# A written-out order for five engines, a ring of three probability groups, and value products in pairs, in an attention and mixture-of-experts kernel

## The chip, the core and the metric

One Trainium2 chip, one core. The metric is device time in microseconds (us) of one execution. TensorE is called PE, VectorE DVE, ScalarE ACT, GpSimd POOL, and SyncE SP; SP issues nearly all transfers.

## The reference, cut to what matters

The input is 8 images of 128 channels by 1024 positions, all float32. Each image ("batch") goes through three stages:

```
x  = x + softmax(q k^T) v                      # one head, key width 16; q,k,v are 1x1 convolutions of x
a  = layernorm(x)                              # token by token
g  = 8-head attention over 1024 tokens (head width 16) of a
l  = 4-head attention over a window of 5 tokens of a
a1 = layernorm(a + silu([g, l] W1) W2);  a2 = layernorm(a1 + silu(a1 W3) W4);  t2 = a2 (with the added t)
```

After all batches every token goes to one of 8 experts (argmax of a gate, capacity 1280 per expert), `relu(x w1 + b1) w2 + b2`, times the gate's probability, is scattered back, and is added to t2.

## The kernel before, in words

The kernel has an opening (weights, the first image's convolution attention), a main stage in which eight batches overlap, a short end for the last batch, and the expert stage with the output. All engines run straight-line programs; what is planned is only the order in which each engine takes its pieces.

A piece is a named **step**, such as `max_pair` or `conv_pv`, with up to four engines that handle it one after the other: for `max_pair` PE fills a PSUM tile and DVE reduces it. `all_steps` (line 584) lists the steps by **chain**: head (convolution attention of a batch, its q, k and the window's rows), maxima, scores, tail (everything behind the attention), local (window attention), and smaller ones. Within a chain an engine keeps the listed order; how the chains are interleaved on an engine is free. Before, `Steps.plan` (line 309) did this at build time with a table of costs (`PARTS`, line 127), a list schedule and one pass that pulls work tight (`justified`); it also put idle matmuls (`end_keep_on`) into gaps of PE at the end.

For the eight-head attention a batch has two **quads** of four heads. Each quad takes 32 `max_pair` steps (line 1602: two fp16 matmuls into `max_ps`, then a DVE reduction over 1024 columns, line 2297), a `guard` that turns the maxima into a row to be subtracted, moved by a transfer (`guard_rows`, lines 1179 and 2309), and then 32 `score_pair` steps (line 1620: two fp16 matmuls into `score_ps`, then one exponential over 1024 columns on ACT into `prob`, line 1994). `max_ps` and `score_ps` are single buffers of two PSUM banks each, so PE can't fill the next pair before DVE or ACT has read this one. Two `score_pair` steps make a **group**: four heads by 512 queries for one block of 128 keys. A `pv_group` (line 1635) multiplies a group with the values: four heads, each on its own 32 columns of the array, float32, 8 matmul records, accumulated over 8 key blocks in `o_ps`; `o_copy` then takes the sum away. `prob` (line 738) holds two groups: the exponential of group g waits for the product of group g - 2 (line 1997).

On PE a batch has, beside these, 16 `conv_max`, 16 `conv_exp` and 8 `conv_pv` (line 1560: 16 matmul records each), 8 `local_qkv`, and the tail's steps (`fuse1`, `fuse2`, `ffn1`, `ffn2` and transposes). On DVE there are 64 maxima and 16 `conv_max` reductions (line 2239) in each batch besides. Head steps share two PSUM banks (three in the opening), tail steps one.

In the opening, ACT's `conv_exp` of the first batch waits for `fold` (line 1917), the last of the weight steps, since the weights are loaded over the tile (`nat`, line 806, inside `cprob`) that the exponentials overwrite. On SP `recall` of batch 0 (line 1132) stands between the two `store_parts` of batch 0 (line 1138), and one `zero_rows` (line 1111: 528 KB of `rows_d` and 512 KB of `y_d`) stands ahead of the first `guard_rows`, the other nine behind it.

Of the kernel before, what the change touches and what calls it, by code (L numbers as in the profile page):

```python
# [19 lines left out]

# [40 lines left out]
GROUPS = 2 * NT  # L61
TILES = GROUPS * QH
# [64 lines left out]
PARTS = {  # L127
    "score_pair": [("pe", 0.26, 0.25), ("act", 1.28, 0.1)],
    "pv_group": [("pe", 1.08, 0.25)],
    "weights": [("sp", 6.0, 9.0)],  # L130
    "weight": [("pe", 0.25, 0.3), ("dve", 0.25, 0.1)],
    "fold": [("pe", 1.6, 0.3), ("dve", 2.0, 0.2), ("act", 0.1, 0.2)],
    "zero_pads": [("sp", 1.8, 3.0)],
    "zero_rows": [("sp", 0.5, 4.0)],
    "o_copy": [("act", 0.55, 0.2)],
    "bounds": [("dve", 1.6, 0.2), ("pe", 0.45, 0.3)],
    "powers": [("dve", 0.5, 0.2), ("pool", 0.4, 0.2)],
    "scales": [("dve", 2.6, 0.2)],
    "max_pair": [("pe", 0.26, 0.25), ("dve", 1.13, 0.1)],
    "guard": [("dve", 0.7, 0.1), ("pe", 0.11, 0.3)],  # L140
    "guard_rows": [("dve", 0.2, 0.2), ("sp", 1.3, 3.5)],
    "load_x": [("sp", 0.4, 9.0)],
    "x_tokens": [("pe", 0.5, 0.3), ("act", 0.55, 0.1)],
    "conv_qk": [("pe", 0.9, 0.3), ("act", 1.12, 0.2), ("dve", 1.38, 0.1)],
    "store_parts": [("sp", 1.3, 4.3)],
    "conv_v": [("pe", 0.87, 0.3), ("dve", 0.6, 0.1)],
    "conv_max": [("pe", 0.22, 0.22), ("dve", 0.6, 0.1)],
    "conv_guard": [("dve", 0.7, 0.1), ("pe", 0.1, 0.3), ("act", 0.3, 0.2), ("sp", 0.7, 2.5)],
    "conv_exp": [("pe", 0.22, 0.22), ("act", 0.54, 0.1)],
    "conv_pv": [("pe", 1.85, 0.25), ("dve", 0.5, 0.1)],  # L150
    "a_channels": [("pe", 0.45, 0.3), ("act", 0.54, 0.1)],
    "keep": [("sp", 1.0, 4.0)],
    "global_qk": [("pe", 0.88, 0.3), ("act", 0.56, 0.2), ("dve", 0.69, 0.1)],
    "local_qkv": [("pe", 0.65, 0.3), ("dve", 0.5, 0.2), ("sp", 0.9, 2.5)],
    "key_stacks": [("sp", 1.9, 4.5)],
    "query_stacks": [("sp", 1.9, 3.2)],
    "global_v": [("pe", 0.88, 0.3), ("dve", 0.6, 0.1)],
    "o_tokens": [("pe", 0.46, 0.3), ("dve", 0.65, 0.1)],
    "o_channels": [("pe", 0.45, 0.3), ("act", 0.54, 0.1)],
    "recall": [("sp", 1.8, 8.0)],  # L160
    "bias": [("pool", 4.9, 0.2)],
    "local_dot": [("sp", 0.9, 6.0), ("pool", 3.6, 0.2)],
    "local_max": [("dve", 2.1, 0.2), ("act", 0.25, 0.2)],
    "local_sum": [("dve", 0.7, 0.2), ("pool", 2.55, 0.2)],
    "local_out": [("pool", 2.8, 0.2)],
    "fuse1": [("pe", 1.73, 0.3), ("act", 1.2, 0.1), ("dve", 0.75, 0.2)],
    "ffn1": [("pe", 0.88, 0.3), ("act", 1.2, 0.1), ("dve", 0.75, 0.2)],
    "fuse2": [("pe", 1.74, 0.3), ("dve", 0.6, 0.1)],
    "ffn2": [("pe", 1.74, 0.3), ("dve", 0.6, 0.1)],
    "stats_t": [("dve", 0.8, 0.1), ("pool", 3.1, 0.1)],  # L170
    "stats_u": [("dve", 0.8, 0.1), ("pool", 3.1, 0.1)],
    "stats_v": [("dve", 0.8, 0.1), ("pool", 3.1, 0.1)],
    "stats_t2": [("dve", 0.8, 0.1), ("pool", 3.1, 0.1)],
    "norm_t": [("act", 1.6, 0.1)],
    "norm_u": [("act", 1.6, 0.1)],
    "affine_u": [("pool", 2.6, 0.1)],
    "norm_v": [("act", 1.6, 0.1), ("pool", 2.6, 0.1)],
    "norm_t2": [("act", 1.6, 0.1)],
    "store_t2": [("sp", 0.4, 3.0)],
    "x1_channels": [("pe", 0.45, 0.3), ("act", 0.54, 0.1)],  # L180
    "n2_channels": [("pe", 0.45, 0.3), ("act", 0.54, 0.1)],
    "logits": [("pe", 1.75, 0.3), ("dve", 1.75, 0.2)],
    "ranks": [("pe", 0.4, 0.3), ("act", 0.3, 0.2), ("dve", 4.2, 0.2)],
    "route": [("pool", 10.2, 3.0)],
    "end_o_tokens": [("pe", 0.46, 0.3), ("dve", 0.65, 0.1)],
    "end_o_channels": [("pe", 0.45, 0.3), ("act", 0.54, 0.1)],
    "end_fuse1": [("pe", 1.73, 0.3), ("act", 0.55, 0.1), ("dve", 1.4, 0.2)],
    "end_fuse2": [("pe", 1.74, 0.3), ("dve", 0.6, 0.1)],
    "end_stats": [("dve", 1.5, 0.1), ("pool", 1.1, 0.1)],
    "end_norm_u": [("dve", 0.9, 0.1)],  # L190
    "end_centre": [("dve", 0.9, 0.1)],
    "end_affine_u": [("pool", 2.6, 0.1)],
    "end_x1_channels": [("pe", 0.45, 0.3), ("act", 0.54, 0.1)],
    "end_ffn1": [("pe", 0.88, 0.3), ("act", 0.55, 0.1), ("dve", 1.4, 0.2)],
    "end_ffn2": [("pe", 1.74, 0.3), ("dve", 0.6, 0.1)],
    "end_norm_v": [("dve", 0.9, 0.1)],
    "end_store": [("sp", 0.4, 3.0)],
    "end_norm_t2": [("dve", 0.9, 0.1)],
    "end_n2_channels": [("pe", 0.45, 0.3), ("act", 0.54, 0.1)],
    "end_logits": [("pe", 0.9, 0.3), ("dve", 1.6, 0.2)],  # L200
    "end_ranks": [("pe", 0.3, 0.3), ("act", 0.3, 0.2), ("dve", 3.2, 0.2)],
    "end_route": [("pool", 1.3, 3.0)],
}

READ_BY_ALL = {"conv_qk", "global_qk"}
BESIDES = {"pe": 0.0, "act": 0.0, "dve": 0.0, "pool": 0.0, "sp": 0.0}
EARLIER = {"head": 0.0, "maxima": 5.0, "scores": 0.0, "tail": 0.0, "local": 1.0}  # L210
TOGETHER = 0.05
GUARD_LANDS = 7.0
STACKS_LAND = 9.0

ZERO_PADS_FROM = 58.0
ZERO_ROWS_FROM = 150.0
FIRST_WEIGHTS, WEIGHTS = 3, 20
SHIFTS = [
]

KEEP_OVER = 0.6
KEEP_SHARE = 0.75
KEEP_EARLY_OVER = 0.35
KEEP_EARLY_SHARE = 0.45
KEEP_TAKES = 0.22
KEEP_AT_END = 40


def first_gap(starts, ends, at, time):

    n, end = 0, len(ends)
    while n < end:
        mid = (n + end) // 2
        if ends[mid] <= at + 1e-9:
            n = mid + 1
        else:
            end = mid
    while n < len(starts) and starts[n] < at + time - 1e-9:
        at = max(at, ends[n])
        n += 1  # L240
    return n, at


def packed(parts, waits, order, backwards):

    taken, at = {}, [0.0] * len(parts)
    for k in order:
        engine, time, arrives = parts[k][:3]
        if backwards:
            t = arrives + max([at[x] + parts[x][1] for x in waits[k]], default=0.0)  # L250
        else:
            t = max([parts[k][5]] + [at[x] + parts[x][1] + parts[x][2] for x in waits[k]])
        starts, ends = taken.setdefault(engine, ([], []))
        n, t = first_gap(starts, ends, t, time)
        starts.insert(n, t)
        ends.insert(n, t + time)
        at[k] = t
    return at


def justified(parts, before, opens, at):

    span = max(t + p[1] + p[2] for t, p in zip(at, parts))
    back = packed(parts, opens, sorted(range(len(parts)), key=lambda k: (-at[k] - parts[k][1], -k)), True)
    late = [span - t - p[1] for t, p in zip(back, parts)]
    return packed(parts, before, sorted(range(len(parts)), key=lambda k: (late[k], k)), False)


def shifted(parts, before, opens, at, what, batch, us):

    key = list(at)
    for k, (_, _, _, (b, step), chain, _) in enumerate(parts):
        if b == batch and what in (step[0], "chain " + chain):
            key[k] += us
        key[k] = max([key[k]] + [key[x] + 1e-6 for x in before[k]])
    at = packed(parts, before, sorted(range(len(parts)), key=lambda k: (key[k], k)), False)
    return justified(parts, before, opens, at)


class Steps:  # L280


    def __init__(self):
        self.steps = []
        self.found = {}
        self.uses = {}
        self.keep_from = None
        self.keeps_on = False
        self.early = False

    def add(self, chain, ahead, step, *before, banks=None, at=0.0):

        n = len(self.steps)
        deps = [(self.found[x], None) for x in before if x in self.found]
# [7 lines left out]
        self.steps.append((chain, ahead, step, deps, held, at))  # L302
# [6 lines left out]
    def plan(self):  # L309

        parts, before = [], []
        part_of, last_in, early, ready = {}, {}, [], []
# [27 lines left out]
        for k, b in enumerate(before):  # L340
            for x in b:
                opens[x].append(k)
# [2370 lines left out]
```

## Time and profile before

| | us |
|---|---|
| median of 3 runs | 1706.99 (1704.41 to 1714.14) |
| profiled execution | 1710.45 |
| its span, first to last instruction | 1708.7 |
| PE / DVE / ACT / POOL busy in the span | 1466.8 / 1251.4 / 994.1 / 715.1 |
| mean granted clock of PE | 0.912 of 2.4 GHz |

Busy time of PE is the union of matmul intervals with modelled ends, so a busy PE may still have room. The share of a whole span mixes stages; the rows further down are by stage.

### The profile page before, as it was taken

How to read it: one execution, taken by the hardware profiler on the slowest of the kernel's cores; microseconds unless marked ns; L12 is line 12 of the kernel's file. 1: busy time of each engine (PE TensorE's matmuls, PEld its weight loads, DVE VectorE, ACT ScalarE, POOL GpSimd, SP SyncE). 2: the span in 40 equal slices, each digit the busy share in tenths (PEclk: the TensorE clock that was granted, in tenths of full speed). 3: DMA queues.
4: the chain of work that ended last, by engine and by line, in shares of the span. 5: the costliest groups of instructions: out<-in, count | busy, mean ns of one | idle time of the engine just before them, and what ended most of it. 6: DMA issues, size and time to landing. Idle time of an engine off the chain costs nothing.

```text
span 1708.7 us, 23938 instructions
## 1 busy us (share of the span) xinstructions
PE 1466.8 (86%) x8489; PEld 691.9 (40%) x8489; DVE 1251.4 (73%) x2245; ACT 994.1 (58%) x1379; POOL 715.1 (42%) x1131
## 2 busy tenths in 40 slices
PE   6767888999999889988998899899978877879993
PEld 4513322543254335333533353245312321449992
DVE  5477688788867886798679867986777732648984
ACT  2302566676667666767576757666665665315543
POOL 5212411145444544454255425542653355224562
PEclk8956799999899999999999999999978965989997
DMA  2234531123212321332034203410421001033335
GB/s 73 95 101 159 193 93 49 40 98 101 81 45 98 98 88 41 101 116 73 35 112 136 72 5 112 147 52 9 157 93 49 35 35 46 7 88 108 107 119 211
DMA packets 111050, 148.40 MB, mean 87 GB/s; under 512 B 13558, under 2 KB 80171, under 8 KB 110932
## 3 DMA queue, kind: packets, MB, share of 16 engines
q1 hardware_dynamic: 103444, 136.69, 24.6%
q0 software_dynamic: 4608, 7.30, 1.3%
q10 hardware_dynamic: 2880, 2.88, 0.5%
q8 instruction: 68, 1.11, 0.3%
q14 instruction: 50, 0.41, 0.1%
HBM read 91.83 MB, written 56.95 MB: 87 GB/s over the span
## 4 chain that ended last, share of the span: by engine, by line
PE 55%; DVE 27%; issue 6%; ACT 6%; POOL 3%; DMA 2%; SPq 1%; POOLq 0%; ACTq 0%; DVEq 0%
DVE gmax L2297 14%; PE bank L1644 10%; PE max_ps L1610 7%; PE bank L1565 7%; PE score_ps L1631 5%; PE bank L1879 4%; PE bank L1681 3%; ACT prob L2000 3%; DVE cmax L2241 3%; PE bank L1671 2%; PE bank L1477 2%; PE bank L1581 2%; DVE stats L2269 2%; PE bank L1557 2%; PE bank L1700 1%
## 5 line engine op out<-in xcount | busy, mean ns | idle before, releaser
L2000 ACT ACTIVATE prob<-score_ps,unscale 128x1024 f32<-128x1024 f32 x512 | 569.3, 1112 | 346.6 <-PE score_ps L1631 345.0
L2297 DVE TENSOR_REDUCE gmax<-max_ps 128x2 f32<-128x1024 f32 x512 | 625.7, 1222 | 165.1 <-PE max_ps L1610 161.1
L1644 PE MATMUL bank<-prob,v_tok 128*32 128x512 f32 x2048 | 306.3, 674 | 1.5 <-ACT prob L2000 1.5
L1610 PE MATMUL max_ps<-arena 48*128 48x512 f16 x1024 | 213.9, 414 | 90.4 <-DVE gmax L2297 78.8
L1631 PE MATMUL score_ps<-arena 50*128 50x512 f16 x1024 | 212.6, 412 | 58.2 <-ACT prob L2000 56.3
L1610 PEld LDWEIGHTS max_ps<-arena 48*128 48x128 f16 x1024 | 50.1, 94 | 311.7 <-DVE gmax L2297 245.2
L1384 POOL TENSOR_TENSOR lprod<-ls,kv_win 128x640 f32<-128x640 f32 x64 | 80.0, 1273 | 227.6 <-DVE ls L2358 227.1
L1377 POOL TENSOR_TENSOR lprod<-ql_tok,kv_win 128x640 f32<-128x640 f32 x64 | 97.8, 1548 | 144.9 <-DMA ql_tok<-ql_d 143.9
L1631 PEld LDWEIGHTS score_ps<-arena 50*128 50x128 f16 x1024 | 50.3, 95 | 211.6 <-ACT prob L2000 159.2
L1565 PE MATMUL bank<-cv_tok,cprob 128*128 128x129 f32 x912 | 116.2, 280 | 1.6 <-DVE t_tok L2264 0.9
L1565 PEld LDWEIGHTS bank<-cv_tok,cprob 128*128 128x128 f32 x912 | 106.4, 191 | 21.8 <-issue 19.2
L1467 POOL DMA_INDIRECT y_d<-kv_win,token_e x80 | 82.6, 1033 | 75.9 <-DVE kv_win L2657 56.1
L1434 POOL DMA_INDIRECT rows_d<-rows,slot x56 | 55.2, 986 | 135.2 <-DVE slot L2457 120.2
L1342 POOL TENSOR_TENSOR mv<-stats 128x4 f32<-128x4 f32 x58 | 11.9, 204 | 197.4 <-DVE stats L2269 197.4
L1644 PEld LDWEIGHTS bank<-prob,v_tok 128*32 128x32 f32 x2048 | 42.2, 112 | 92.4 <-issue 81.2
L2241 DVE TENSOR_REDUCE cmax<-bank 128x1 f32<-128x512 f32 x107 | 71.9, 682 | 2.1 <-PE bank L1543 2.1
L1955 ACT ACTIVATE cprob<-bank 128x512 f32<-128x512 f32 x110 | 64.2, 597 | 9.9 <-PE bank L1557 9.8
L1351 POOL TENSOR_TENSOR rstd<-mv,half_pow 128x4 f32<-128x4 f32 x58 | 59.0, 1018 | 4.6
L1543 PE MATMUL bank<-ck_stack,cq_stack 128*128 128x512 f32 x107 | 56.3, 540 | 3.6 <-DVE cmax L2241 3.3
L2027 ACT ACTIVATE tanh_t<-bank,hcols 128x512 f32<-128x512 f32 x56 | 38.4, 687 | 32.1 <-PE bank L1671 20.9
L2363 DVE SCALAR_TENSOR_TENSOR hid<-tanh_t,half_t 128x512 f32<-128x512 f32 x56 | 48.3, 862 | 9.2 <-ACT half_t L1909 9.2
L1586 PE MATMUL bank<-lT,a_cm 128*128 128x384 f32 x118 | 54.7, 553 | 0.0
(399 smaller groups left out, 2496.7 us busy)
## 6 DMA issues: line engine op xcount, KB each, us to landing
kv_win<-kv_d SPq DMA_DIRECT2D x32, 1280.0 KB, 5.5
kv_d<-lqkv SPq DMA_DIRECT2D x64, 128.0 KB, 1.8
arena<-gparts_d SPq DMA_DIRECT2D x96, 64.0 KB, 2.6
rows_d<-rows SPq DMA_DIRECT2D x10, 528.0 KB, 6.9
cprob<-rows_d SPq DMA_DIRECT2D x8, 660.0 KB, 5.8
x_cm<-in_x_dram SPq DMA_DIRECT2D x8, 512.0 KB, 3.3
kept_d<-t_tok SPq DMA_DIRECT2D x8, 512.0 KB, 2.6
kept_d<-a_tok SPq DMA_DIRECT2D x8, 512.0 KB, 3.6
```

Of the source, the lines that this page charges most:

```text
L1377: m = pool.tensor_tensor(lprod[:, i, :, :], ql_tok[:, i, None, :].to_broadcast([P, WIN, C]), kv_win[:, i, :, 0:C], ALU.mult)
L1384: m = pool.tensor_tensor(lprod[:, i, :, :].rearrange("p w (h d) -> p w h d", d=LD), ls[:, i, :, :, None].to_broadcast([P, WIN, LH, LD]), k ...
L1467: pool.indirect_dma_start(y_d, bass.IndirectOffsetOnAxis(ap=token_e[e % 2][:, i:i + 1], axis=0), y_e[e % 2][:, i, :], None, bounds_check=l ...
L1565: last = mm(ps[:, 0:C + 1], conv_prob(b, i // HT)[:, j, (i % HT) * P:(i % HT + 1) * P], cv_tok[:, j, :], start=(j == 0), stop=(j == NT - 1))
L1610: last = mm(max_ps[:, z, :], q_stack[quad][Z * z:Z * z + CROWS, r, i * P:(i + 1) * P], key_slot(b, quad)[Z * z:Z * z + CROWS, r, j * HN:(j ...
L1631: last = mm(score_ps[:, z, :], key_slot(b, quad)[Z * z:Z * z + KM, r, j * P:(j + 1) * P], q_stack[quad][Z * z:Z * z + KM, r, half * HN:(ha ...
L1644: last = mm(o_ps[CG * h:CG * (h + 1), :], v_tok[:, j, quad * QH + h, :], prob[:, g % 2, h, :], start=(j == 0), stop=(j == NT - 1))
L1879: last = mm(bank[6 + u % 2][:, i * C:(i + 1) * C], hid_e[f][:, lo + i * P:lo + (i + 1) * P], w2_e[e % 2][:, f, :], start=(f == 0), stop=(f ...
L1955: nc.scalar.activation(conv_prob(b, h)[:, j, :], ps[:, :], ACT.Exp).then_inc(free, 1)
L2000: nc.scalar.activation(prob[:, g % 2, 2 * r:2 * r + 2, :], score_ps[:, :, :], ACT.Exp, scale=unscale[:, quad * PAIRS + r:quad * PAIRS + r ...
L2241: v.tensor_reduce(cmax[:, t // 2, t % 2:t % 2 + 1], ps[:, :], AX.X, ALU.max)\
L2297: v.tensor_reduce(gmax[:, :, r * NT + i, j:j + 1], max_ps[:, :, :], AX.X, ALU.max).then_inc(max_free, 1)
```

## The change

1. The planner with its costs goes. A table `ORDER` gives, for each engine, one letter per step: the chain whose next step the engine takes. `Steps.orders` expands it, `Steps.check` walks it once at build time. Idle matmuls at the end are the dots: 69 single ones in place of 12 steps of 3 to 21.
2. `prob` holds three groups (`PROB_RING = 3`), used in turn across quads and batches.
3. One `pv_group` takes two adjacent key blocks (`VALUES = 2`): 16 matmul records in a row, 8 such steps for each quad and 16 for each batch; they form a chain of their own, `values`. The exponential of group g now waits for the step that holds group g - 3.
4. `nat` moves from `cprob` to a part of `arena` that isn't used yet; `conv_exp` of batch 0 no longer waits for `fold`.
5. The early idle matmuls are deleted from the code (the order before holds none of them).

With the table some steps pass others on a queue. On SP, `recall` of batch 0 now stands behind both `store_parts`, and seven `zero_rows` stand ahead of the first `guard_rows`. On DVE the 16 `conv_max` of batch 1 come among the first twenty maxima, and the 8 `conv_pv` of batch 1 ahead of the first guard (four of them came behind it before).

```diff
+PROB_RING = 3
+VALUES = 2
+PRODUCTS = GROUPS // VALUES
...
+CHAINS = {"h": "head", "m": "maxima", "s": "scores", "t": "tail", "l": "local", "p": "split", "q": "queries",
+          "k": "keys", "x": "x", "z": "zero", "a": "end0", "b": "end1", "v": "values"}
+
+ORDER = {
+    "pe": (
+        "hhhhhhhhxhxhxhhhhhhhhhhhhhxxxxxxxxxxxxxhhhhhxhhhxhhhhhhhhhhxhhhhhhhhhhhhhhhthhhhthmhmmhmhmmhmhhmhhh"
+        "mhhhhhhhmhhmhhmhmmmhmmhhmhhhmhhhmhmhmhmhmhhmmmhhmhhmhhmhhmhhmhmmmhmhhmshmshmshmshmsvsmhhsmsmshmsvsmh"
...
+        "stmsmsvmstmsmstmsvmtsmtststsvstssssvsssvssstsvtstsstssvsssvssssvasasaasasaasvsasbbv...babaabba..b...."
+        "............b...bb..........ba...a...................ab...b..........b"
+    ),
...
+    "sp": (
+        "xxxhzhpptqkhhqxhhkhhqhhqlhlzzzzzzzmzhzzlppkxhhhhqlhhhhmqkhlqmhqppkxhhlhhqhhhlhmqkhttqlqmhlppkxlhhhhh"
...
-                      (a, ("pv_group", quad, n // PAIRS - 2)), banks=SCORE_PS)
-        if n % PAIRS == PAIRS - 1 and n >= PAIRS:
-            product(n // PAIRS - 1)
-    product(GROUPS - 1)
+        s.add("scores", a, ("score_pair", quad, n), (a, ("guard_rows", quad)), group(n // PAIRS - PROB_RING),
+              banks=SCORE_PS)
+        if (n + 1) % (VALUES * PAIRS) == 0:
+            product((n + 1) // (VALUES * PAIRS) - 1)
...
-        prob = sb("prob", [P, 2, QH, HN])
+        prob = sb("prob", [P, PROB_RING, QH, HN])
...
-        nat = cprob[:, :, :].rearrange("p a b -> p (a b)")
+        nat = arena[:, (QUADS + KEY_SLOTS) * N:]
...
+                for g in range(n * VALUES, (n + 1) * VALUES):
+                    j = g % NT
+                    for h in range(QH):
+                        last = mm(o_ps[CG * h:CG * (h + 1), :], v_tok[:, j, quad * QH + h, :], prob_of(b, quad, g)[:, h, :],
+                                  start=(j == 0), stop=(j == NT - 1))
...
-                if r == 0 and not (isinstance(b, int) and b == 0 and quad == 0 and g < 2):
-
-                    after(act, pv_made, b * 2 * GROUPS + quad * GROUPS + g - 1)
+                if r == 0:
+
+                    after(act, pv_made, ((2 * b + quad) * GROUPS + g - PROB_RING) // VALUES + 1)
```

## Rows read from the trace of the kernel before

**Rows 1.** Busy time by stage: stretch, its length, PE, PEld, DVE, ACT, POOL, clock, DMA.

```profile
0.00:89.00 89.00, 60.88 (x291) 42.21 (x291) 39.60 (x105) 24.89 (x45) 33.55 (x67) 0.87 0.30 88
89.00:163.00 74.00, 53.16 (x172) 21.83 (x170) 59.41 (x78) 4.66 (x10) 11.27 (x9) 0.58 0.32 105
...
784.00:951.00 167.00, 151.47 (x908) 65.17 (x908) 134.31 (x234) 114.06 (x159) 77.88 (x134) 0.98 0.25 83
...
1289.00:1424.00 135.00, 108.37 (x578) 35.39 (x578) 73.40 (x133) 86.94 (x111) 64.27 (x105) 0.80 0.15 49
...
1540.00:1662.00 122.00, 122.00 (x909) 114.52 (x908) 106.37 (x210) 62.43 (x114) 69.64 (x68) 1.00 0.39 115
```

**Rows 2.** Maxima (line 2297) and exponentials (line 2000): min/median/max ns, first and last start.

```profile
L2297 DVE TENSOR_REDUCE gmax<-max_ps x512: 1206/1225/1229, 89.5 to 1375.3; 128x2 f32<-128x1024 f32 x171
...
L2000 ACT ACTIVATE prob<-score_ps,unscale x512: 1092/1113/1137, 163.1 to 1462.7; 128x1024 f32<-128x1024 f32 x171
```

**Rows 3.** Waits in 453 to 1118 us: engine, line, releaser; total us, times, longest.

```profile
ACT prob L2000 <- PE score_ps L1631: 164.7, 148, 8.5
PEld max_ps L1610 <- DVE gmax L2297: 106.1, 148, 1.7
```

**Rows 4.** PE's timeline at full clock: start, us, line; turns, and a product alone.

```profile
254.14 0.39 PE L1610 MATMUL max_ps<-arena 48*128 48x512 f16 x2 [0.33 <-DVE gmax L2297]
254.37 0.38 PE L1631 MATMUL score_ps<-arena 50*128 50x512 f16 x2
254.68 0.91 PE L1586 MATMUL bank<-lT,a_cm 128*128 128x384 f32 x2
255.85 0.39 PE L1610 MATMUL max_ps<-arena 48*128 48x512 f16 x2 [0.27 <-DVE gmax L2297]
...
759.54 1.06 PE L1644 MATMUL bank<-prob,v_tok 128*32 128x512 f32 x8
760.54 0.39 PE L1631 MATMUL score_ps<-arena 50*128 50x512 f16 x2
```

**Rows 5.** PE's timeline: products side by side, and two alone at low clock.

```profile
1305.21 3.59 PE L1644 MATMUL bank<-prob,v_tok 128*32 128x512 f32 x16
...
1464.19 1.92 PE L1644 MATMUL bank<-prob,v_tok 128*32 128x512 f32 x16
...
1410.15 1.93 PE L1644 MATMUL bank<-prob,v_tok 128*32 128x512 f32 x8
...
1413.84 0.61 PE L1631 MATMUL score_ps<-arena 50*128 50x512 f16 x2 [1.21 <-ACT prob L2000]
1414.38 1.93 PE L1644 MATMUL bank<-prob,v_tok 128*32 128x512 f32 x8
```

**Rows 6.** DVE by line and shape, whole span: the reduction of `conv_max`.

```profile
L2241 DVE TENSOR_REDUCE cmax<-bank 128x1 f32<-128x512 f32 x107 | 71.9, 682 | 2.1 <-PE bank L1543 2.1
```

**Rows 7.** The chain of waits in the opening: start, us, what.

```profile
29.95 0.27 PE score_ps L1477
...
36.51 0.79 PE score_ps L1557
...
76.07 8.46 DMA gparts_d<-parts
```

**Rows 8.** SP's queue: start, us to issue, line, transfer.

```profile
73.43 0.64 SPq L1135 DMA_DIRECT2D t_old<-kept_d  x1
74.11 1.23 SPq L1136 DMA_DIRECT2D a_old<-kept_d  x1
75.44 1.31 SPq L1142 DMA_DIRECT2D gparts_d<-parts  x2
...
155.70 1.39 SPq L1183 DMA_DIRECT2D arena<-gneg_rows  x2
157.14 0.41 SPq L1113 DMA_DIRECT2D rows_d<-rows  x1
```

**Rows 9.** Busy time while zero rows are written; the last two columns DMA share, GB/s.

```profile
160.00:170.00 10.00, 7.48 (x42) 2.96 (x40) 8.68 (x18) 5.20 (x7) 3.25 (x12) 0.76 1.01 331
```

More of the change, by code:

```diff
@@ L21 @@
+from collections import deque
 from contextlib import ExitStack
@@ L120 @@
 TAIL_TURNS = len(TAIL_USES)
[L127 to L202, printed above, removed]
@@ new lines @@
+ENGINES = {
+    "load_x": "sp",
+    "weights": "sp",
+    "weight": "pe dve",
+    "fold": "pe dve",
+    "bounds": "dve pe",
+    "powers": "dve pool",
+    "scales": "dve",
+    "zero_pads": "sp",
+    "zero_rows": "sp",
+    "conv_qk": "pe act dve",
+    "x_tokens": "pe act",
+    "conv_v": "pe dve",
+    "conv_max": "pe dve",
+    "conv_guard": "dve pe act sp",
+    "conv_exp": "pe act",
+    "conv_pv": "pe dve",
+    "stats_t": "dve pool",
+    "norm_t": "act",
+    "keep": "sp",
+    "a_channels": "pe act",
+    "global_qk": "pe act dve",
+    "store_parts": "sp",
+    "query_stacks": "sp",
+    "key_stacks": "sp",
+    "global_v": "pe dve",
+    "local_qkv": "pe dve sp",
+    "max_pair": "pe dve",
+    "guard": "dve pe",
+    "guard_rows": "dve sp",
+    "local_dot": "sp pool",
+    "local_max": "dve act",
+    "local_sum": "dve pool",
+    "local_out": "pool",
+    "score_pair": "pe act",
+    "pv_group": "pe",
+    "o_copy": "act",
+    "o_tokens": "pe dve",
+    "recall": "sp",
+    "o_channels": "pe act",
+    "bias": "pool",
+    "fuse1": "pe act dve",
+    "fuse2": "pe dve",
+    "stats_u": "dve pool",
+    "norm_u": "act",
+    "affine_u": "pool",
+    "x1_channels": "pe act",
+    "ffn1": "pe act dve",
+    "ffn2": "pe dve",
+    "stats_v": "dve pool",
+    "norm_v": "act pool",
+    "stats_t2": "dve pool",
+    "norm_t2": "act",
+    "store_t2": "sp",
+    "n2_channels": "pe act",
+    "logits": "pe dve",
+    "ranks": "pe act dve",
+    "route": "pool",
+    "end_o_tokens": "pe dve",
+    "end_o_channels": "pe act",
+    "end_fuse1": "pe act dve",
+    "end_fuse2": "pe dve",
+    "end_stats": "dve pool",
+    "end_norm_u": "dve",
+    "end_affine_u": "pool",
+    "end_x1_channels": "pe act",
+    "end_ffn1": "pe act dve",
+    "end_ffn2": "pe dve",
+    "end_centre": "dve",
+    "end_norm_v": "dve",
+    "end_store": "sp",
+    "end_norm_t2": "dve",
+    "end_n2_channels": "pe act",
+    "end_logits": "pe dve",
+    "end_ranks": "pe act dve",
+    "end_route": "pool",
@@ L203 @@
 }
 READ_BY_ALL = {"conv_qk", "global_qk"}
[L209 to L216, printed above, removed]
-FIRST_WEIGHTS, WEIGHTS = 3, 20
[L218 to L225, printed above, removed]
-KEEP_AT_END = 40
[L229 to L241, printed above, removed]
@@ L244, in packed @@
[L244 to L258, printed above, removed]
@@ L261, in justified @@
[L261 to L277, printed above, removed]
+FIRST_WEIGHTS, WEIGHTS = 3, 20
@@ L286, in __init__, with add @@
         self.uses = {}
[L287 to L291, printed above, removed]
+    def add(self, chain, ahead, step, *before, banks=None):
         n = len(self.steps)
-        deps = [(self.found[x], None) for x in before if x in self.found]
+        deps = [self.found[x] for x in before if x in self.found]
         held = None
@@ L301, in add @@
             uses.append(n)
-        self.steps.append((chain, ahead, step, deps, held, at))
+        self.steps.append((chain, ahead, step, deps, held))
         self.found[ahead, step] = n
@@ new lines, in orders @@
+    def orders(self):
+        ahead = {}
+        for n, (chain, _, step, _, _) in enumerate(self.steps):
+            for engine in ENGINES[step[0]].split():
+                ahead.setdefault((engine, chain), deque()).append(n)
+        orders = {}
+        for engine, chains in ORDER.items():
+            orders[engine] = [ahead[engine, CHAINS[c]].popleft() if c != "." else None for c in chains]
+        assert not any(ahead.values())
+        self.check(orders)
+        last = self.steps[0]
+        named = {}
+        for engine, order in orders.items():
+            named[engine] = []
+            for n in order:
+                last = self.steps[n] if n is not None else (None, last[1], ("end_keep_on", 1))
+                named[engine].append((last[1], last[2]))
+        return named
@@ new lines, in check @@
+    def check(self, orders):
+        at = {engine: 0 for engine in orders}
+        done = [0] * len(self.steps)
+        moved = True
+        while moved:
+            moved = False
+            for engine, order in orders.items():
+                while at[engine] < len(order):
+                    n = order[at[engine]]
+                    if n is not None:
+                        _, _, step, deps, held = self.steps[n]
+                        engines = ENGINES[step[0]].split()
+                        if engines[done[n]] != engine:
+                            break
+                        if any(done[d] < len(ENGINES[self.steps[d][2][0]].split()) for d in deps):
+                            break
+                        if engine == "pe" and held is not None:
+                            by = len(ENGINES[self.steps[held][2][0]].split())
+                            if done[held] < (by if self.steps[held][2][0] in READ_BY_ALL else min(2, by)):
+                                break
+                        done[n] += 1
+                    at[engine] += 1
+                    moved = True
+        assert all(at[engine] == len(order) for engine, order in orders.items())
@@ L633, in all_steps @@
         end_of_half(s, B - 1, h)
-    s.keep_from = (B - 1, ("pv_group", 1, GROUPS - 1))
-    return s.plan(), s.turns("head")
+    return s.orders(), s.turns("head")
 def hybrid_kernel(nc, x, wq, bq, wk, bk, wv, bv, g_in_w, g_in_b, g_out_w, g_out_b, t_in_w, t_in_b, t_out_w,
@@ L1814, in end_ranks @@
                 mm(ps[:, HT * E:2 * HT * E], ones[:, :], oh, start=True, stop=True).then_inc(full, 1)
-            def early_keep_on(b, count):
-                for _ in range(count):
-                    mm(o_ps[:, :], identh[:, :], identh[:, None, :].to_broadcast([P, HT, P]), start=True, stop=True)
             def end_keep_on(b, count):
@@ L2287, in global_v @@
                 if h == 0:
-                    after(dve, pv_made, b * 2 * GROUPS)
+                    after(dve, pv_made, b * 2 * PRODUCTS)
                 v.tensor_tensor(v_tok[:, HT * h:HT * h + HT, :, 0:D],
```

167 lines of the change are left out of this document (77 added, 90 removed).

## The prediction

> **What bounds the kernel now.** I read busy time by stage first [rows 1]. The experts (1540 to 1662 us) keep PE busy all the time at full clock, and nothing in the change touches them. In a middle batch (784 to 951 us) PE is busy 151.5 of 167 us and DVE 134.3, so two engines are nearly full and neither is quite. From 89 to 163 us DVE is the busier (59.4 of 74) and PE runs at clock 0.58; in the last batch (1289 to 1424) ACT with 86.9 of 135 and PE with 108.4 at clock 0.80 share it. So the bound changes by stage, and what is missing is overlap, which is what an order can give.
>
> The waits say why [rows 3]: ACT's exponentials wait for PE's scores, and PE's next maximum for DVE's reduction. Both are single buffers, handed to and fro. I call the time from one `max_pair` on PE to the next a **turn**; there are 512, the first reduction starts at 89.5 us and the last at 1375.3 [rows 2], so the turns fill 1285.8 us, three quarters of everything. A turn can't be shorter than about 1.72 us, since PE waits for DVE even with a piece of other work in it (254.14 to 255.85) [rows 4].
>
> **The change part by part.** To compare the two orders I expanded both into steps and priced them alike: PE's steps by the distance to the next start in its timeline where it doesn't idle (a score 0.31, a product alone 1.00 [rows 4]), DVE's by the means of their rows (a maximum 1.23 [rows 2], a `conv_max` 0.68 [rows 6]; chains of small operations as the sum of theirs). These are sums of rows; they don't follow semaphores.
>
> *Products in pairs.* A product alone takes PE 1.00 us until the next start (759.54 to 760.54), with 1.06 of busy time [rows 4]. Two in a row have 1.92 of busy time at full clock [rows 5], so 1.86 to the next start: 0.14 less than two alone. 128 pairs give 18 us of PE's work, of 1148 before the end stage.
>
> That isn't all gain. The pair is one piece that nothing can be put into. In a turn with scores alone, a single product (1.00) hides beneath the exponential (1.11 [rows 2]); a pair (1.86) doesn't, so PE comes 0.75 late to the next score. At the lower of its two clock levels (1.2 of 2.4 GHz) it is 3.59 against an exponential of 1.11 [rows 5]. The ring of three lets ACT run one group further while a pair is pending; the table places 114 of 128 pairs a turn or two behind the last score that they need, so their own wait is nothing, covered by the following score's exponential. If that cover goes, each of the other 14 pays an exponential, 1.1 us, at most 15 in all. What is queued behind such a wait on PE is the next maximum; DVE would wait for that.
>
> *The order.* Per turn I took the largest of PE's work, DVE's work and 1.72, and summed. If nothing could run ahead, each turn would pay its own largest: 1288 before, 1302 after. If the two engines may average over two turns: 1242 and 1217; over four: 1214 and 1168; over eight: 1172 and 1127. So after spreads its work more evenly, but has more single turns that are too short or too long (turns with less than 0.7 of PE work: 62 against 32). Measured were 1285.8 [rows 2], near the first sum, but the sums hold no low clock, and PE's clock is under 1 in nearly every stage [rows 1]. How far PE runs ahead is set by its free PSUM tiles: one for maxima, two for the head, one for the tail, some two turns of steps. I take the middle between two turns (25 us less) and four (46 less): **36 us less**. The ends are 14 more and 46 less.
>
> *The opening.* Before, the first exponential's matmul starts at 36.51, behind the weights' last step, though the guard of the convolution was transposed at 29.95 [rows 7]. Its transfer is some 3 us, so 2 to 4 us can go. Then `recall` moves behind both stores: SP spends 73.43 to 75.34 on its two transfers and only then issues the second store [rows 8], which takes 8.46 us to land with that megabyte about [rows 7]; the first maximum waits for what is read back. This gives 2 us of issue and perhaps as much in landing. Behind `recall` the first query stack now waits for SP, but it needs the first store landed, which takes longer. Together the first maximum comes 0 to 12 us earlier; I take **7.5**.
>
> *Between there and the first score*, DVE's steps from the first maximum to the first of the second quad sum to 66.8 us instead of 58.5, since batch 1's `conv_pv` and statistics come ahead of the guard. This is inside the turns' sum.
>
> *Zero rows.* Seven pairs of them, 7.3 MB, now stand on SP ahead of the first `guard_rows` (before: one; the guard is issued at 155.70, the next at 157.14 [rows 8]). At the 331 GB/s of the stretch that is full of them [rows 9] they take 22 us. The window steps that SP waits on before them fall after the twentieth maximum, and some 25 us of DVE's work stand between that and the guard. So I cost it at nothing, hidden by those maxima; if that cover is short, at most 7 us. The Trainium skill ("DMA: Bandwidth & Descriptors", Queues, rings and completion order) says that each DMA engine consumes the descriptors of one ring in order, and SP has one ring on each. By that rule the guard's 8 KB, if issued right behind the zeros, would land 22 us late, and the forecast below would be 22 us higher; no run here shows that case yet.
>
> *The last quad.* No maxima are left there. Taking per score the larger of PE's work and its loop of 1.65 us (0.39 of PE, 1.11 of ACT, hand-over), I get 59.2 after and 55.6 before: **3.6 more**. At the low clock that the rows at 1410 us show, two turns take 4.23 (1410.15 to 1414.38 [rows 5]), four 8.5; with a pair of 3.59 they would take 9.5, so at most 9 more for 8 pairs.
>
> *At nothing*: the deleted early idle matmuls (none were issued), 69 single idle matmuls for the 83 in the end's gaps, ACT's dropped wait. They only fill PE's own gaps.
>
> Sum: 36 + 7.5 - 3.6, some 40 us less. From 1710.45, the profiled execution, this gives 1670.5; the median stands 3.5 below that execution, so **1667**.
>
> **The rivals.**
> *More comes of it (chance 0.22).* The two late stages run at clock 0.58 and 0.80 [rows 1]. If the evener order lifts the last batch from 0.80 to 0.95, PE's 108 us there become 91, and with the full four-turn gain (46) and the opening's 12 the sum is 17 + 46 + 12 - 3.6, or 71 less: 1636. For it: PE is the busiest engine there. Against: with few steps left the loops set the pace.
> *Lockstep (0.16, the other side).* DVE and ACT can't run ahead, every turn pays its own largest, and the pair of 1.86 or 3.59 us is longer than anything that could hide it. Place: turns with little other work, and the last quad. Price: 14 + 9 - 7.5, 15.5 us slower: 1722. It decides as soon as PE's lead is below two turns. For it: measured time lies on the one-turn sum. Against: that sum would leave nothing for the low clock.
> *The gain is given back (0.12).* Two-turn averaging (25 less) and the opening (7.5), but 7 from the guard behind the zeros, 9 in the last quad, and some 10 of the waits of pairs set right behind their exponential: about 7 less, 1700, no change that can be told.
>
> **How the numbers follow.** About 0.5% (8.5 us) is what a measurement of this kernel can tell from no change. The forecast (0.50) and the first rival are faster: 0.72. The third is the same: 0.12. Lockstep is slower: 0.16. The likeliest case alone spans 1645 to 1698. The range goes to 1630, just past the first rival, and up to 1722, the price of lockstep, which leaves about 2 in 10 out.
>
> **What would show it.** PE busy should fall by some 18 us; products should come as 16 records with 1.92 us of busy time. The 512 maxima should span about 1250 us instead of 1285.8, with the first near 82. ACT's waits for scores and PE's for maxima [rows 3] should fall together. The guard's transfer should be out before PE asks for the first score. Wrong would be: a middle batch still at 167 us, pairs at 3.59 in many places, or a span of the maxima above 1285.8 with DVE waiting longer for PE.

## The result, and the profile after

The changed kernel takes 1731.2 us (median of 4 runs, 1722.5 to 1733.5) where the kernel before took 1706.9 beside it: a ratio of 1.0126, 95% interval 1.0079 to 1.0173. It is slower by 1.3%, and the forecast was 1667, faster. The profiled execution takes 1732.84 us with a span of 1731.1, so 22.4 us more of span than that of the kernel before.

Busy time by stage of the kernel after, in the stretches of [rows 1] and with the same columns:

```profile
0.00:89.00 89.00, 60.14 (x292) 41.20 (x292) 40.18 (x105) 25.10 (x45) 31.36 (x66) 0.88 0.30 84
89.00:163.00 74.00, 56.69 (x206) 28.69 (x207) 57.66 (x83) 10.84 (x23) 16.51 (x22) 0.66 0.46 153
784.00:951.00 167.00, 145.88 (x823) 59.99 (x823) 132.24 (x212) 106.30 (x143) 74.38 (x108) 0.89 0.25 82
1289.00:1424.00 135.00, 107.92 (x593) 37.23 (x586) 89.64 (x142) 82.15 (x104) 56.67 (x82) 0.84 0.16 55
1540.00:1662.00 122.00, 116.22 (x819) 104.80 (x818) 89.95 (x177) 57.82 (x105) 59.48 (x59) 0.97 0.39 113
```

The column to read is the granted clock, third from the end of each line. From 784 to 951 us it was 0.98 before and is 0.89 now. The clock has two levels, so a mean of 0.89 says that about a fifth of the stretch ran at 1.2 GHz. This is the stretch of these rows that lost most. All middle batches together ran at 0.98 before, as the next line shows, and run at 0.93 now (the same line of after stands below, with the first run that has idle matmuls):

```profile
453.00:1118.00 665.00, 602.35 (x3630) 259.51 (x3629) 538.25 (x926) 457.30 (x632) 312.46 (x536) 0.98 0.25 83
```

From 89 to 163 us the clock rose, from 0.58 to 0.66, and over the whole span it went only from 0.912 to 0.904. (The last line of the first block differs for another reason: the experts start later, and the stretch still holds some of the end.)

Maxima and exponentials after, each line with its first and last start as in [rows 2]; below them the products by line, whose mean is the second number behind the bar:

```profile
L2271 DVE TENSOR_REDUCE gmax<-max_ps x512: 1203/1226/1229, 89.2 to 1412.0; 128x2 f32<-128x1024 f32 x171
...
L1974 ACT ACTIVATE prob<-score_ps,unscale x512: 1088/1113/1155, 178.4 to 1494.1; 128x1024 f32<-128x1024 f32 x171
...
L1626 PE MATMUL bank<-prob,v_tok 128*32 128x512 f32 x2048 | 301.1, 714 | 1.5 <-ACT prob L1974 1.5
```

So the 22.4 us are put together like this. The first exponential starts at 178.4 instead of 163.1: 15.3 later. From the first to the last one it takes 1315.7 us instead of 1299.6: 16.1 more. Behind the last one 237.0 are left instead of 246.0: 9.0 less. The 512 maxima span 1322.8 us instead of 1285.8. The last line answers a smaller question: PE practically never idles before a pair until an exponential ends (1.5 us in all).

### The profile page after: what moved, and what is told of

Same layout as the page of the kernel before. It is cut to its first block, busy times and chain, and to the rows that moved or that the text cites. A ratio compares the mean times of both kernels' runs of the same rounds, so it can differ in the third digit from the quotient of the medians.

```text
span 1731.1 us, 23908 instructions
## 1 busy us (share of the span) xinstructions
PE 1460.4 (84%) x8475; PEld 713.5 (41%) x8475; DVE 1268.8 (73%) x2245; ACT 993.0 (57%) x1379; POOL 717.3 (41%) x1131
## 3 DMA queue, kind: packets, MB, share of 16 engines
q10 hardware_dynamic: 2880, 2.88, 0.5%
q8 instruction: 68, 1.11, 0.3%
## 4 chain that ended last, share of the span: by engine, by line
PE 55%; DVE 25%; ACT 9%; issue 5%; POOL 3%; DMA 2%; SPq 1%; POOLq 0%; ACTq 0%; DVEq 0%
PE bank L1626 14%; DVE gmax L2271 13%; PE max_ps L1591 6%; PE bank L1546 6%; ACT prob L1974 5%; PE score_ps L1612 5%; PE bank L1856 4%; PE bank L1663 3%; DVE cmax L2215 3%; PE bank L1653 3%; PE bank L1458 2%; PE bank L1567 1%; DVE hid L2337 1%; PE bank L1562 1%; PE bank L1695 1%
## 5 line engine op out<-in xcount | busy, mean ns | idle before, releaser
L1626 PE MATMUL bank<-prob,v_tok 128*32 128x512 f32 x2048 | 301.1, 714 | 1.5 <-ACT prob L1974 1.5
L1626 PEld LDWEIGHTS bank<-prob,v_tok 128*32 128x32 f32 x2048 | 59.8, 123 | 150.2 <-issue 145.2
L1538 PE MATMUL bank<-cq_stack,ck_stack 128*128 128x512 f32 x110 | 52.7, 520 | 1.4 <-ACT cprob L1929 0.6
## 6 DMA issues: line engine op xcount, KB each, us to landing
kv_win<-kv_d SPq DMA_DIRECT2D x32, 1280.0 KB, 5.5
```

Of the source, the lines that this page charges most:

```text
L1626: last = mm(o_ps[CG * h:CG * (h + 1), :], v_tok[:, j, quad * QH + h, :], prob_of(b, quad, g)[:, h, :], start=(j == 0), stop=(j == NT - 1))
```

## What the pair meets

PE's timeline in the kernel after, around 323 us (start, us, line, what, and the idle time before it):

```profile
321.53 0.39 PE L1612 MATMUL score_ps<-arena 50*128 50x512 f16 x2 [0.99 <-ACT prob L1974]
321.87 0.39 PE L1591 MATMUL max_ps<-arena 48*128 48x512 f16 x2
323.13 0.39 PE L1612 MATMUL score_ps<-arena 50*128 50x512 f16 x2 [0.88 <-ACT prob L1974]
323.58 0.39 PE L1591 MATMUL max_ps<-arena 48*128 48x512 f16 x2
324.73 0.61 PE L1612 MATMUL score_ps<-arena 50*128 50x512 f16 x2 [0.76 <-ACT prob L1974]
325.29 0.61 PE L1591 MATMUL max_ps<-arena 48*128 48x512 f16 x2
325.83 3.64 PE L1626 MATMUL bank<-prob,v_tok 128*32 128x512 f32 x16
329.40 0.61 PE L1591 MATMUL max_ps<-arena 48*128 48x512 f16 x2
```

Three turns hold only a score and a maximum, and PE is idle for about half of each. At 324.73 the score takes 0.61 instead of 0.39: the clock has gone to its lower level. The pair comes right then and takes 3.64 us instead of 1.92. Of the 128 pairs, 92 take 1.92 or 1.93, as in [rows 5]; the other 36 take 2.4 to 3.64. Before, 38 of the 246 products that stood alone took over a fifth longer than at full clock. Two things are in this picture, and the experiments had to part them: a piece twice as long in a queue that goes in order (theory L, the lump), and bare turns that let the clock fall (theory C). A third was left: the new table is a worse order whatever stands in it (theory B; theory A is that the pair costs in any order).

For some expectations I walked through the written lists: each engine takes its steps in order, a step starts when its engine is free and what it needs is done, 0.06 us for each hand-over, the prediction's prices, full clock throughout. Its results are estimates. Between the first and the last maximum it gives 1297 us for the old order and 1288 for the new one.

In the orders below, one letter is one step on PE: `m` a `max_pair`, `s` a `score_pair`, `v` a product (single or pair), `h` a step of the next batch's head, `t` of the tail of the batch before.

## The experiments

**The old order, single products, and all else of the change.** The ring of three groups, the staging array in the arena and the dropped waits, with the order of before as a table.

```
-VALUES = 2
+VALUES = 1
-ORDER: after's five lists
+ORDER: the five lists that the planner of before gives
```

> The order of before, written out as a table, with single products; of the change only the ring of three groups, the staging array moved into the arena and the two dropped waits are in it. If the pair is what costs (theory A, a piece of 1.86 us at full clock or 3.6 us at the low one): 1700 to 1707 us, no pair, no cost. If the new order is what costs (theory B): 1700 to 1707 us as well. If the ring itself costs (an exponential that runs further ahead takes ACT or PSUM at a bad moment): 1720 or more.

Measured: 1709.1 us against 1708.4, ratio 1.0002 (0.9981 to 1.0023). This is 2 us above what theories A and B had, and 11 below what a ring that costs would have given. The ring, the array and the waits do nothing that can be told, either way. What is left is the order and the pair.

**The old order, products in pairs.** The second `v` of two becomes the pair, the first goes; PE's list from the 150th score on:

```
-svhmthshmtsmvhmhstmshvsmhsvshmsvshhtsvmvmsthmshhmstmsvmtmsht
+svhmthshmtsmhmhstmshvsmhsshmsvshhtsmvmsthmshhmstmsmtmshtmstv
```

> The order of before with the products merged: each pair stands where the second of its two singles stood, everything else as before. Theory A (the pair costs, whatever the order): 1725 to 1735 us, the whole loss, with the low clock in about as many stretches as after. Theory B (the new order costs, the pair is worth its 0.14 us per pair or nothing): 1690 to 1707 us.

Measured: 1821.3 us, ratio 1.0648 (1.0621 to 1.0676), 113 us slower. No theory had so much. The engines around one pair of this kernel, from the timelines of PE, DVE and ACT:

```profile
799.65 0.39 PE L1612 MATMUL score_ps<-arena 50*128 50x512 f16 x2 [0.76 <-ACT prob L1974]
...
802.78 0.61 PE L1591 MATMUL max_ps<-arena 48*128 48x512 f16 x2 [0.81 <-DVE gmax L2271]
803.31 3.64 PE L1626 MATMUL bank<-prob,v_tok 128*32 128x512 f32 x16
806.89 0.61 PE L1612 MATMUL score_ps<-arena 50*128 50x512 f16 x2
...
803.43 1.23 DVE L2271 TENSOR_REDUCE gmax<-max_ps 128x2 f32<-128x1024 f32 x1 [0.25 <-PE max_ps L1591]
807.96 1.23 DVE L2271 TENSOR_REDUCE gmax<-max_ps 128x2 f32<-128x1024 f32 x1 [3.31 <-PE max_ps L1591]
...
807.54 1.11 ACT L1974 ACTIVATE prob<-score_ps,unscale 128x1024 f32<-128x1024 f32 x1 [4.42 <-PE score_ps L1612]
```

While PE works on the pair, the next score and the next maximum stand behind it in its queue; ACT is idle for 4.42 us and DVE for 3.31. At full clock it is the same in small: at 1075.74 a pair of 1.92 leaves DVE idle for 1.17.

How much a pair lengthens its turn can be counted over many turns. I put the starts of `max_pair` and of products on PE side by side (200 to 1300 us) and took the mean time from one `max_pair` to the next, with the number of turns in brackets:

| kernel | turns without a product | with one single | with a pair |
|---|---|---|---|
| old order, ring of three, singles | 2.19 us (232) | 2.68 (189) | |
| old order, pairs | 2.28 (302) | | 4.08 (90) |
| after (new order, pairs) | 2.26 (315) | | 3.66 (105) |

A single adds 0.49, so half of its 1.0 us is hidden. A pair adds 1.80 in the old order and 1.40 in the new one, both more than the 0.98 of two singles. How much more depends on where a turn is taken to begin: counted from one reduction on DVE to the next, a single adds 0.37 and a pair 1.11 and 1.07. So the table shows that a pair sticks out more than two singles do, and not its exact price; the price is the 113 us of the whole kernel. These means hold the low clock too.

**The new order, single products.** The second single stands where the pair stood, the first two scores earlier (in 6 cases one):

```
-stmshhmstmsvmstsmhhsmhsvmsmhsmsmhsmsmvhsmhhsmhsvsmhhsmhsmhsm
+stmsvhhmstmsvmstsvmhhsmhsvmsmhsmsvmhsmsmvhsvmhhsmhsvsmhhsvmh
```

> The order of after with every pair taken apart again: the second single stands where the pair stood, the first two scores earlier (122 pairs) or one score earlier (6). Theory A: back to 1700 to 1710 us, since the long piece is gone. Theory B: 1725 to 1745 us, since all other steps stand where after has them.

Measured: 1772.8 us, ratio 1.0357 (1.0323 to 1.0391), slower than after by more than theory B had. So neither the pair nor the new order is bad by itself in the same way everywhere: pairs cost 113 us in the one order, and taking them apart costs 42 in the other. Two causes are in the 42 us, and no run parts them. PE now idles 27.1 us before products (1.5 in after), 15.9 of them until an exponential ends: 168 of the 256 singles stand one score behind the last that they need, where 240 stood two behind in the old order. And a single may be pushed into a turn that is already full, which is argued here and not shown. The walk has this sign (the new order with these singles 1342, the old one with pairs 1331); measured are 1368.0 and 1391.7.

**The new opening, then the old order with pairs.**

```
-ORDER: the old lists throughout
+ORDER: after's lists up to the first score_pair, then the old lists without the steps already done
```

> The order of after on every engine up to the first score, and from there the order of before with merged products; of what after does early (half of the second batch's convolution) nothing is done twice. Against the run with the old order throughout and pairs: if the opening's 15.3 us are lost for good (theory B, first part), 10 to 16 us slower; if they are only work done earlier (8 conv_exp, 4 conv_pv, two a_channels and four of global_qk's matmul groups moved ahead), 0 to 4 us slower, and the loss is in the later stages.

Measured: 1834.5 us, ratio 1.0726 (1.0699 to 1.0753), so 13 us more than the old opening with the same order and pairs. In the profiled executions the first exponential comes 9.5 us later (174.2 against 164.7), and from the first to the last one it takes 1411.7 us instead of 1413.9. So of what after does early, half of the second batch's convolution, next to nothing is given back.

**After with idle matmuls.** They add zeros to the products' sums while these are open, and stand where the walk leaves PE idle (`,` is one such matmul, 0.2 us):

```
+def idle(b, count):
+    mm(o_ps[:, :], idle0[:, :], identh[:, None, :].to_broadcast([P, HT, P]), start=False, stop=False)
-stmshhmstmsvmstsmhhsmhsvmsmhsmsmhsmsmvhsmhhsmhsvsmhhsm
+st,mshh,mstmsvmstsmhhsm,hsvmsmh,s,,,,ms,,,,,m,hs,,ms,,,mvhsmhhsmhsvsmhhsm
```

> After, with 499 more matmuls that add zeros to the open sums of the products, placed where a walk through the three engines' lists with the row prices leaves PE idle; their results change nothing. Theory C (the low clock is what the turn sums missed: the walk at full clock makes after 10 us faster than before, and after has 31 us more of low clock than before, 333.6 against 303.1): the low clock between 200 and 1480 us falls by more than half and the time goes to 1695 to 1715 us. Theory L (only the lump of sixteen and the in-order queues): 1731 to 1745 us, the clock makes no difference to a loop that waits.

Measured: 1705.4 us, ratio 0.9975 (0.9959 to 0.999), 26 us less than after, with 499 matmuls more and nothing else moved. Middle batches and the last batch of this kernel:

```profile
453.00:1118.00 665.00, 622.94 (x3724) 277.94 (x3723) 537.53 (x916) 443.61 (x612) 307.42 (x526) 0.97 0.25 82
1289.00:1424.00 135.00, 119.96 (x708) 44.22 (x700) 81.58 (x140) 87.72 (x112) 64.90 (x105) 0.97 0.14 49
```

and the first of these stretches in after itself:

```profile
453.00:1118.00 665.00, 591.99 (x3474) 259.96 (x3473) 535.39 (x900) 442.13 (x609) 299.78 (x500) 0.93 0.24 80
```

The clock rises from 0.93 to 0.97, and from 0.84 to 0.97 in the last batch; over 200 to 1480 us it rises from 0.91 to 0.97, so the part at the lower level falls from some 18% to 6%, more than by half. Time and clock are as theory C had them. Only 14 of the 128 pairs are slowed now instead of 36. So raising the clock was worth 26 us to after, net of the time that the added matmuls take. How much of after's loss that explains depends on what the old order gains by the same means, two runs below. The Trainium skill ("TensorE: Matmul & The Clock Gate", A second HAM failure mode: psum-queue depth-cycling) describes a kernel whose PE is idle for moments between groups of matmuls, again and again, and whose clock swings between its two levels; the fall at 324.73 agrees, behind idle moments of 0.76 to 0.99 us.

**The old order with pairs and idle matmuls** (592 of them):

```
-svhmthshmtsmhmhstmshvsmhsshmsvshhtsmvmsthmshh
+svhmthshmtsm,h,,,mhstmshvsmhs,,,,,,s,,hmsvshhts,,,,,m,,,vmsthmshh
```

> The order of before with merged products, with 592 of the same zero matmuls. A walk at full clock makes merged products cost this order 33 us, measured were 106 between the first and the last maximum. Theory C: the low clock falls from 450 us to under 350 and the time from 1821 to 1770 to 1790 us. Theory L: 1815 to 1840 us.

Measured: 1769.3 us, ratio 1.0346 (1.032 to 1.0372), 0.7 us below the range of theory C. The low clock falls to some 220 us, worked out from the mean clock below.

**The old order with single products and idle matmuls** (532, placed in the same way):

```
-svhmthshmtsmvhmhstmshvsmhsvshmsvshhtsvmvmsthmshhmst
+svhmthshmtsmvh,mhstmshvs,,m,hsv,,,,,s,,hmsvs,hhtsv,,,,,mvmsthmshhmst
```

> The order of before with single products and the ring of three, with 532 of the same zero matmuls. Theory C: its late batches run at 0.80 of the clock, so 1680 to 1700 us, faster than both kernels. Theory L: 1708 to 1720 us.

Measured: 1699.0 us, ratio 0.9938 (0.9919 to 0.9957). Mean granted clock of the three kernels with idle matmuls (new order, old order with pairs, old order with singles), in this order; without them they had 0.904, 0.877 and 0.916:

```profile
core 0: 1703.8 us, clock 0.940
```

```profile
core 0: 1763.8 us, clock 0.937
```

```profile
core 0: 1696.7 us, clock 0.957
```

Raising the clock takes 26, 52 and some 10 us off the three. But between the old order with pairs and with singles, both with a clock near full, 70 us are left, so the pairs' 113 us are about 43 of clock and 70 of lump (some of the 70 may still be clock, since 0.937 isn't 0.957). Theory L and theory C both hold, and neither alone. The new order with pairs was 22 us slower than the old one with singles (1731.2 against 1709.1) and is 6 us slower with the clock up in both (1705.4 against 1699.0): some 16 of the 22 go with the clock.

**Pairs cut in two, at the same place.**

```
-stmshhmstmsvmstsmhhsmhsvmsmhsmsmhsmsmvhsmhhsmhsvsmhhsmhs
+stmshhmstmsvvmstsmhhsmhsvvmsmhsmsmhsmsmvvhsmhhsmhsvvsmhhsmhs
```

> After with each pair as two steps of eight that stand one behind the other at the pair's place: the order of everything else and the length of PE's piece stay, only the first step no longer waits for the second group's exponentials and frees its ring slot earlier. If the joint wait and the late release of two slots cost (theory W): under 1715 us. If it is the length of the piece and the place (theories L and C): 1728 to 1742 us.

Measured: 1730.9 us, ratio 1.0109 (1.0085 to 1.0132), the same as after. That one step waits for two groups and frees two of three slots together costs nothing; theory W falls. What is left is that PE has the work of two products, 16 records, in one place.

**Idle matmuls in the opening too**, for both orders:

```
 old order, singles
-hhhhhhhhhhhhthhhhhthmhmmhmhmmhmmhmhhmhm
+hhhh;;;;;;;;;;;;;;;;;;;;hhhhhhhhth;;hhhht;;;;;;;;;;;;;;h;;;;;;;mh;m;;;;mh;m;;hm;;;m;hm;;;m;;hmhh;mh;;m
```

(`;` starts a sum in the bank that no product uses yet.)

> The order of before with single products and the 532 zero matmuls of the earlier run, and 122 more idle matmuls between the weights' last step and the first score, where the clock was 0.58. If the opening is held by PE at the low clock (theory C): the first score comes 4 to 10 us earlier than 165.0 and the time is 1688 to 1696 us. If the opening is held by DVE and by transfers: 1697 to 1702 us, no change against that run.

> After with its 499 zero matmuls and 110 more ahead of its first score. With the clock up throughout, the two orders differ by the opening alone: half of the second batch's convolution (14 us of PE's work at full clock) lies ahead of the first score. Theory O (what is done early isn't given back, as the run with the new opening and the old order had it): first score 8 to 14 us later than in the other run of this call, time 5 to 12 us longer. If the low clock made the opening longer: first score under 5 us later and the same time within 4 us.

Measured: 1688.6 us (ratio 0.9874, 0.9843 to 0.9904) for the old order with singles, and 1695.8 (0.9923, 0.9893 to 0.9953) for the new order with pairs. From 89 to 163 us, the old order first, and the exponentials and maxima of both:

```profile
89.00:163.00 74.00, 60.24 (x271) 23.77 (x271) 63.92 (x91) 10.75 (x19) 15.18 (x21) 0.96 0.42 138
...
L1988 ACT ACTIVATE prob<-score_ps,unscale x512: 1092/1114/1137, 155.5 to 1441.9; 128x1024 f32<-128x1024 f32 x171
L2285 DVE TENSOR_REDUCE gmax<-max_ps x512: 1204/1225/1229, 88.7 to 1359.7; 128x2 f32<-128x1024 f32 x171
```

```profile
89.00:163.00 74.00, 64.59 (x312) 31.85 (x310) 61.46 (x98) 12.39 (x28) 18.52 (x33) 0.94 0.50 166
...
L1986 ACT ACTIVATE prob<-score_ps,unscale x512: 1089/1114/1156, 166.8 to 1450.3; 128x1024 f32<-128x1024 f32 x171
L2283 DVE TENSOR_REDUCE gmax<-max_ps x512: 1205/1226/1229, 86.4 to 1373.8; 128x2 f32<-128x1024 f32 x171
```

The opening's clock goes from 0.58 to 0.96 in the old order, and its first exponential comes at 155.5 instead of 165.0, as theory C had it. The new order's comes 11.3 us later than that and its time is 7.2 us longer, as theory O had it. These lines are the cleanest comparison of the two orders. From the first exponential to the last the new one takes 1283.5 us instead of 1286.4, and it has 239.5 us of span behind the last instead of 245.7. (This execution of the new order lies 4.2 us below its median, so the 3 us are within the scatter.) The 512 maxima, which are the turns that the prediction summed, span 1287.4 us in the new order and 1271.0 in the old one: 16.4 more. So the late opening is hardly made good: with the clock up in both, the new order gains next to nothing from the first exponential to the last, and is 7 us slower as a whole. The old order with the ring, single products and all idle matmuls beats both kernels, by 1.3% against before.

## Why the prediction was wrong

**Products in pairs**: the work was right, the price was not. At full clock a pair has 1.92 us of busy time as the step had it. But 18 us less of PE's work was to come, and PE's busy time fell by only 6.4, from 1466.8 to 1460.4; the products' own row fell by 5.2, from 306.3 to 301.1, with 36 of the 128 pairs slowed by the lower clock. The sentence that a pair doesn't hide beneath an exponential, so that PE comes 0.75 late, named the right thing and got no price of its own; 128 times 0.75 is 96, and the lump in the old order measured some 70. That the pair's own wait is covered was right (1.5 us).

**The order** is the step that failed. It took 36 us less, a middle between two turns and four over which PE and DVE might average. Measured, the maxima's span grew by 37 us (1322.8 against 1285.8). Two things were wrong in the step. First, there is next to no averaging: with the clock up in both, the maxima's span is 1287.4 against 1271.0, 16 us more. That is nearest to the sum in which each turn pays its own largest (14 more), and far from that of two turns (25 less) and that of four (46 less). Of the 16, 13.6 lie between the first maximum and the first exponential; the exponentials' span itself is 3 us less. Second, the prediction said that its sums hold no low clock and then used their difference as if the clock were the same in both. It wasn't: 0.93 against 0.98 in the middle batches. Raising it gave 26 us to after against some 10 to the old order, and of the 37 us that the maxima's span grew some 21 are gone with the clock up.

The prediction had the sign of this in hand. It counted turns with less than 0.7 us of PE's work, 62 after and 32 before, and took them for turns that are too short only. The rows at 323 us show the clock falling in such turns, and matmuls that fill them raise it.

The waits of [rows 3] seem to show what the prediction wanted to see. In the same stretch of the kernel after they are:

```profile
ACT prob L1974 <- PE score_ps L1612: 154.9, 138, 4.7
PEld max_ps L1591 <- DVE gmax L2271: 91.4, 135, 2.3
```

That is 10 and 15 us less, but the stretch of 665 us now holds 247 exponentials instead of 257. For each exponential ACT waits 0.63 us instead of 0.64, and PE waits 0.37 instead of 0.41 for maxima. A stretch of fixed length can't show a gain when the work in it slides out. What did come is the sign that was to speak against the forecast: a maxima's span above 1285.8 us with DVE waiting longer for PE. Over the whole span, before and after:

```profile
DVE gmax L2297 <- PE max_ps L1610: 161.1, 198, 2.6
```

```profile
DVE gmax L2271 <- PE max_ps L1591: 184.2, 232, 4.2
```

**The opening**: 7.5 us earlier were taken, 0.3 came (89.2 against 89.5). PE's timeline after shows the convolution's exponentials at 34.40 instead of 36.51, but the weights' last step then stands among them:

```profile
34.40 0.77 PE L1538 MATMUL score_ps<-cq_stack,ck_stack 128*128 128x512 f32 x1
...
38.74 1.91 PE L1482 MATMUL bank<-hid,arena 128*128 128x256 f32 x4
...
42.12 0.74 PE L1538 MATMUL score_ps<-cq_stack,ck_stack 128*128 128x512 f32 x2 [0.46 <-DVE hcols L2138]
```

and on SP, as in [rows 8], the store comes first and the load of query stacks behind it:

```profile
74.89 1.44 SPq L1123 DMA_DIRECT2D gparts_d<-parts  x2
76.37 1.16 SPq L1116 DMA_DIRECT2D t_old<-kept_d  x1
77.57 1.40 SPq L1117 DMA_DIRECT2D a_old<-kept_d  x1
79.01 5.22 SPq L1141 DMA_DIRECT2D arena<-gparts_d  x8
...
169.93 1.43 SPq L1164 DMA_DIRECT2D arena<-gneg_rows  x2
```

In the chain of waits the store lands 2.1 us earlier than in [rows 7], but the last load that the first maximum needs takes 4.48 us now instead of 2.88 (before, then after):

```profile
85.90 2.88 DMA arena<-gparts_d
```

```profile
75.50 6.95 DMA gparts_d<-parts
83.80 4.48 DMA arena<-gparts_d
```

**Between the first maximum and the first score** 15.6 us were added (89.2 against 73.6, to the first exponential). The step saw 8.3 us of added DVE work and left it inside the turns' sum. The run with the new opening and the old order shows that hardly any of it is given back (13 us slower as a whole), and the last two runs show it again (the first score 11 us later, the time 7 longer). What the other 7 of the 15.6 us are stays open.

**Zero rows** at nothing: right, as far as the trace shows. The guard was issued at 169.93, when DMA had fallen idle; its share (tenths) over 160 to 171 us:

```profile
DMA  9999999999999999999989999996200000000000
```

The rule of the Trainium skill that the prediction weighed ("DMA: Bandwidth & Descriptors", Queues, rings and completion order), that descriptors of one ring are consumed in order, would have delayed a guard issued right behind the zeros. This one was issued some 2 us after they had drained, so no run here decides the rule.

**The last quad** was taken at 3.6 us more; its 31 turns take 72.8 us instead of 72.9. Behind the last exponential 9.0 us came back, on which the prediction had nothing. It comes with the new order: the other runs with it have 236 to 240 us there, those with the old one 244 to 246.

**The rivals.** Lockstep had the right mechanism and gave 1722, 9 us short of what came. That it came so near is partly luck: its 14 us for the turns are the 16 measured at full clock, but its 9 us for the last quad and its 7.5 for the opening did not come, the clock's share was missing, and the 9.0 behind the last exponential stood in no term. The prediction gave it 0.16, with the argument that a one-turn sum would leave nothing for the low clock. That argument fell because the sums were a little high: for the old order the sum was 1288, and with the clock up it measured 1271.0. "More comes of it" called 0.58 and 0.80 the clock of two late stages, but 0.58 is the opening's; the last batch's clock did rise, from 0.80 to 0.84, while the middle batches lost more. Of the terms of "The gain is given back" none came: the guard wasn't delayed, the last quad didn't grow, and pairs hardly waited for exponentials. The range ended at 1722 and missed by 9 us.

**What stays open.** With the clock near full, the walk is still some 17 us too high for the old order with singles (1297 against 1280.0, in the runs without idle matmuls in the opening), and 10 too low for the two kernels with pairs: 1331 against 1341.4 for the old order, 1288 against 1297.8 for the new one. So pairs cost some 27 us more than the walk has, about 0.2 us for each pair, and no run says where. A new order that keeps the old opening wasn't tried.

## What to carry to other kernels

Where engines hand single buffers to and fro, price an order turn by turn first, and let turns average only if a run shows that they do; here the sum without averaging came nearest. A step that is made twice as long can cost what it sticks out of its turn, even if it saves work. Count the turns that leave PE nearly bare in both versions, because the clock that falls in them slows the next long piece; in such turns matmuls that change nothing can make a kernel faster. Work moved ahead of a serial loop is lost unless the loop's turns get shorter by it. And compare waits for each piece of work, not for each stretch of time.

## What the hardware showed that was not expected

PE busier by instructions that do nothing made every kernel faster that got them: from 1460.4 to 1521.2 us of PE busy time and 26 us off the time of after. Before the fall shown at 324.73, PE had been idle for 0.99, 0.88 and 0.76 us in three turns running, and the mean clock of the middle batches went from 0.98 to 0.93. The matmuls that raised it again had zeros as one operand.
